# Causal attention row maxima: six reductions per group over pairs of PSUM banks in place of twelve over single banks

## The reference

```python
q = bitlinear(x, wq).reshape(B, S, N_KV, G, HEAD_DIM)
k = bitlinear(x, wk).reshape(B, S, N_KV, HEAD_DIM)
v = bitlinear(x, wv).reshape(B, S, N_KV, HEAD_DIM)
scores = jnp.einsum('bskgd,btkd->bkgst', q, k) * sm_scale
scores = jnp.where(causal, scores, -jnp.inf)
probs = jax.nn.softmax(scores, axis=-1)
out = jnp.einsum('bkgst,btkd->bskgd', probs, v)
```

## Time and profile before

| | |
|---|---|
| time, median of 3 runs | 691.62 us (690.61 to 692.38) |
| span of the profiled execution (first to last instruction) | 690.5 us |
| PE busy | 581.9 us, 84% |
| DVE busy | 451.5 us, 65% |
| ACT busy | 311.6 us, 45% |
| POOL busy | 251.7 us, 36% |
| mean granted TensorE clock | 0.938 of 2.4 GHz |

### The profile page before, as it was taken

One profiled execution on the slowest core, in us unless ns is written; L12 is line 12 of the kernel. 1 busy time (PEld: TensorE's weight loads), 2 busy tenths in 40 slices (PEclk: granted clock), 3 DMA queues, 4 the chain that ended last, 5 costly groups with the idle time before them and its releaser, 6 DMA issues.

```text
span 690.5 us, 11130 instructions
## 1 busy us (share of the span) xinstructions
PE 581.9 (84%) x3618; PEld 420.6 (61%) x3618; DVE 451.5 (65%) x881; ACT 311.6 (45%) x511; POOL 251.7 (36%) x294
## 2 busy tenths in 40 slices
PE   0358999999998897988626879998989989999994
PEld 0244544554443486766524667886768868888883
DVE  5898767877773667555888658758675464444444
ACT  1132556666676532275115563433534444444442
POOL 5821233343447314031030632443324434444440
PEclk9976599999999999999768989999999999999998
DMA  6063210111330013000020112231222222222310
GB/s 171 0 162 97 59 38 22 34 35 36 112 111 1 12 47 58 0 1 1 0 91 0 47 47 68 84 101 46 69 69 78 89 82 80 88 89 90 91 54 30
DMA packets 25627, 41.22 MB, mean 60 GB/s; under 512 B 3640, under 2 KB 17272, under 8 KB 25592
## 3 DMA queue, kind: packets, MB, share of 16 engines
q1 hardware_dynamic: 25160, 39.72, 19.5%
q0 software_dynamic: 432, 1.05, 0.9%
HBM read 37.81 MB, written 3.80 MB: 60 GB/s over the span
## 4 chain that ended last, share of the span: by engine, by line
PE 57%; DVE 25%; issue 7%; ACT 6%; POOL 3%; DMA 1%; SPq 1%; POOLq 0%; DVEq 0%; ACTq 0%
PE ps L1484 9%; PE ps L1472 7%; PE ps L1473 7%; PE ps L1474 7%; PE ps L1424 7%; PE ps L1553 6%; PE ps L1435 6%; PE ps L1427 2%; DVE st L756 2%; DVE xn L684 2%; ACT h_hi L1246 2%; DVE hf L1100 2%; DVE sg L1095 2%; PE ps L1680 1%; DVE negm L844 1%
## 5 line engine op out<-in xcount | busy, mean ns | idle before, releaser
L638 POOL TENSOR_TENSOR mslot_lo<-mraw,mslot_hi 128x768 fp32r<-128x768 f32 x60 | 112.2, 1870 | 176.7 <-ACT mslot_hi L1298 176.7
L844 DVE TENSOR_REDUCE negm<-ps 128x1 f32<-128x512 f32 (+2 forms) x192 | 107.6, 593 | 36.7 <-PE ps L1427 35.6
L1246 ACT CAST h_hi<-hf 128x512 fp32r<-128x512 f32 x76 | 47.2, 621 | 181.3 <-DVE hf L1100 144.1
L1208 ACT ACTIVATE probs<-ps 128x512 f32<-128x512 f32 x160 | 91.9, 597 | 66.7 <-PE ps L1435 66.0
L1472 PE MATMUL ps<-cols_hi,mslot_hi 128*128 128x512 f32 x240 | 96.4, 402 | 3.7 <-ACT sg L1240 2.2
L1473 PE MATMUL ps<-cols_hi,mslot_lo 128*128 128x512 f32 x240 | 94.3, 393 | 0.0
L1474 PE MATMUL ps<-cols_lo,mslot_hi 128*128 128x512 f32 x240 | 93.7, 390 | 0.0
L1095 DVE TENSOR_TENSOR sg<-sg,ps 128x512 f32<-128x512 f32 x60 | 41.0, 683 | 75.0 <-PE ps L1474 58.3
L1484 PE MATMUL ps<-mslot_hi,h_hi 128*128 128x256 f32 x240 | 78.0, 325 | 9.0 <-DVE h_lo L1104 9.0
L1424 PE MATMUL ps<-k_all,q_all 72*128 (+4 forms) x256 | 73.8, 330 | 9.2 <-DMA q_all<-q_parts_scratch 7.4
L1104 DVE TENSOR_TENSOR h_lo<-hf,h_hi 128x512 fp32r<-128x512 f32 x60 | 41.5, 692 | 41.2 <-ACT h_hi L1246 41.2
(11 more groups left out here) (221 smaller groups left out, 1176.7 us busy)
## 6 DMA issues: line engine op xcount, KB each, us to landing
mraw<-in_moe_w SPq DMA_DIRECT2D x60, 384.0 KB, 3.1
q_all<-q_parts_scratch SPq DMA_DIRECT2D x48, 96.0 KB
q_parts_scratch<-qparts SPq DMA_DIRECT2D x6, 256.0 KB, 2.5
k_parts_scratch<-kparts SPq DMA_DIRECT2D x6, 192.0 KB, 3.8
k_all<-k_parts_scratch SPq DMA_DIRECT2D x6, 192.0 KB
xa<-in_x SPq DMA_DIRECT2D x2, 512.0 KB, 4.9
w2a<-in_w SPq DMA_DIRECT2D x1, 1024.0 KB, 8.0
w1raw<-in_w SPq DMA_DIRECT2D x2, 512.0 KB, 5.4
```

Source lines behind the costliest of these rows:

```text
L638: pool.tensor_tensor(mslot_lo[:, place, :], mraw[:, place, :], mslot_hi[:, place, :].bitcast(F32), ALU.subtract)\
L844: dve.tensor_reduce(negm[:, par, qt, h0:h0 + nh], ps[:, u % 4, 0:nh * w].rearrange("p (h t) -> p h t", h=nh), AX.X, ALU.max, negate=True). ...
L1208: act.activation(probs[:, par, u, :], ps[:, 4 + u % 2, :], ACT.Exp)\
L1246: act.copy(h_hi[:, par, :], hf[:, par, :]).then_inc(h_hi_done, 1)
```

## The change

`UNITS` now has six entries, each for four heads of tiles 1 and 0 or two heads of tiles 3 and 2. PE makes them at even u only, and each fills two banks: the four banks are a ring of two pairs, and R of pair j waits until pair j-2 has been reduced. DVE makes one reduction over both banks of a pair, at even u. Everything else stands where it stood. In the loop, PE has six waits on `s1_read` fewer per slot, and DVE six waits and six reductions fewer.

```diff
-        UNITS = ([(3, h, 1) for h in range(4)] + [(2, h, 1) for h in range(4)]
-                 + [(1, 0, 2), (1, 2, 2), (0, 0, 2), (0, 2, 2)])
+        UNITS = [(3, 0, 1), (3, 2, 1), (2, 0, 1), (2, 2, 1), (1, 0, 2), (0, 0, 2)]
+        ROW_UNITS = len(UNITS)
...
-                    need(pool, s1_read, g * 12 + 12)
+                    need(pool, s1_read, (g + 1) * ROW_UNITS)
...
-                for u, (qt, h0, nh) in enumerate(UNITS):
-                    if has(n, 0):
+                for u in range(12):
+                    if has(n, 0) and u % 2 == 0:
                         g = n
+                        pair_of, (qt, h0, each) = u // 2 % 2, UNITS[u // 2]
                         if u == 0:
                             need(dve, msplit, g - 1)
-                        need(dve, s1_full, g * 12 + u + 1)
+                        need(dve, s1_full, g * ROW_UNITS + u // 2 + 1)
                         w = (qt + 1) * P
                         dve.tensor_reduce(
-                            negm[:, par, qt, h0:h0 + nh],
-                            ps[:, u % 4, 0:nh * w].rearrange("p (h t) -> p h t", h=nh),
+                            negm[:, par, qt, h0:h0 + 2 * each]
+                            .rearrange("p (k h) -> p k h", k=2),
+                            ps[:, 2 * pair_of:2 * pair_of + 2, 0:each * w]
+                            .rearrange("p k (h t) -> p k h t", h=each),
                             AX.X, ALU.max, negate=True).then_inc(s1_read, 1)
...
             def score_rows(g, u):
-                qt, h0, nh = UNITS[u]
-                need(pe, s1_read, g * 12 + u - 3)
+                qt, h0, each = UNITS[u]
+                need(pe, s1_read, g * ROW_UNITS + u - 1)
                 w = (qt + 1) * P
-                for h in range(h0, h0 + nh):
-                    c = (h - h0) * w
-                    pe.matmul(ps[:, u % 4, c:c + w],
+                for h in range(h0, h0 + 2 * each):
+                    bank, c = 2 * (u % 2) + (h - h0) // each, (h - h0) % each * w
+                    pe.matmul(ps[:, bank, c:c + w],
...
-                        score_rows(g, u)
+                        if u % 2 == 0:
+                            score_rows(g, u // 2)
```

More of the change, by code:

```diff
@@ L1418, in score_rows @@
             def score_rows(g, u):
-                qt, h0, nh = UNITS[u]
-                need(pe, s1_read, g * 12 + u - 3)
+                qt, h0, each = UNITS[u]
+                need(pe, s1_read, g * ROW_UNITS + u - 1)
                 w = (qt + 1) * P
-                for h in range(h0, h0 + nh):
-                    c = (h - h0) * w
-                    pe.matmul(ps[:, u % 4, c:c + w],
+                for h in range(h0, h0 + 2 * each):
+                    bank, c = 2 * (u % 2) + (h - h0) // each, (h - h0) % each * w
+                    pe.matmul(ps[:, bank, c:c + w],
                               q_all[0:72, bass.ds(g * (GQ * T) + (h * T + qt * P), P)],
                               k_all[0:72, bass.ds(g * T, w)], start=True, stop=False)
-                    mm = pe.matmul(ps[:, u % 4, c + w - P:c + w], identb[:, :], hide_cols[:, :],
+                    mm = pe.matmul(ps[:, bank, c + w - P:c + w], identb[:, :], hide_cols[:, :],
                                    start=False, stop=True)
@@ L1539, in slot @@
                         pe.wait_ge(att_ready, NKV)
-                        pe.wait_ge(s1_read, 12 * NG)
+                        pe.wait_ge(s1_read, ROW_UNITS * NG)
                         transposes(0, 0, att_tile(0))
```

## The result

The changed kernel takes 697.72 us (median of 4 runs, 696.05 to 698.12) beside 691.48 us of before (4 runs, 690.61 to 692.38): ratio 1.0082, 95% interval 1.0067 to 1.0098, +6.2 us. The profiled execution has a span of 696.0 us where before had 690.5, so it is 5.5 us longer.

The account below looks back on a forecast made before the run. PE was taken to bound the steady slots, DVE and PE's chain to `mrow` slots 0 and 1. Steady slots +4.0 us and the head +1.0 made +5.0 on the 691.6 median: 696.6 us, range 692.0 to 699.5.

Parts of the forecast that it names:

- What bounds the kernel: Steady slots: PE is busy 14.94 of 15 us, DVE has 3.5 us to spare; a faster DVE alone gives nothing.
- DVE's busy total: Whole kernel: a sign to look for, DVE's busy total falling by 8 to 14 us while the time does not.
- The price of a two-bank reduction: DVE: a pair of 1,024 elements costs between 1.07 and 1.20 us, taken as 1.14 start to start, 1.22 in duration.
- rival C: Pairs stop PE if a two-bank reduction lasts 1.7 us, not 1.22; at 2.4 us each, 709 us; chance 8%.
- The steady slots, +4.0 us: Slots 4 to 15 and the second cast: PE meets ACT later, 0.31 us a loop slot; bounds 1.2 and 6.5.
- R never waits for DVE from slot 2 on: PE from slot 2 on: a sign to look for, score rows never held by DVE's reductions.
- the ring's 0.4 us to spare: Tightest place, tile 3's second pair: DVE reads it until 3.4 us, R wants its banks at 3.85; cost 0.
- Slots 0 and 1, +1.0 us: Head: later Hadamard product and whole pairs delay `mrow`, so slot 2 begins at 68.5, was 67.47; bounds 0.5 and 2.2.
- less if the clock rises within it: Head: the Hadamard product takes 3.57 us at the half clock, less with a rise within it; end 58.8 to 59.3.
- 1.6 if the clock does not rise during the Hadamard product: Head: a bound on the loss in slots 0 and 1, 1.6 us where the forecast has +1.0.
- A (no change): Rival: ACT's stops do not add up, the loop keeps 9.77 us; only slots 0 and 1 cost, 692.6 us; chance 20%.
- B (PE's sequencer): Rival: PE's register work lengthens loop slots, six fewer waits per slot help; -2.8 us, 688.8 us; chance 9%.

Follow-up runs that it names:

- e2: Kernel before with only PE's order changed to two units at each even step; DVE keeps twelve single reductions: 695.76 us, ratio 1.0056.
- e1: Kernel before with only DVE's reductions made in pairs; PE keeps one unit per step: 694.90 us, ratio 1.0047.
- e3: Changed kernel with the last two heads of query tile 0 put back behind PV3: 696.67 us, ratio 1.0079.
- e7: Changed kernel with DVE's copy `v_now` moved behind the first reduction of a slot: 696.86 us, ratio 1.0077.
- e10: Kernel before with the whole change (pairs on PE and DVE) in slots 0 and 1 only: 693.24 us, ratio 1.0032.
- e4: Kernel before with the whole change from slot 2 on; slots 0 and 1 as before: 695.13 us, ratio 1.0063.
- e9: Kernel before with, up to slot 15, PV0 to PV3 at steps 5 to 8 and division, `o_cols` and `v_now` moved: 690.26 us, ratio 0.9988.
- e5: Changed kernel with the Hadamard product of slot 0 one step earlier, ahead of the fourth pair: 697.82 us, ratio 1.0087.
- e6: Kernel before with DVE's reductions in pairs, PE's old order, and `v_now` moved behind a slot's first reduction: 694.41 us, ratio 1.0042.
- e8: Kernel before with PV0 to PV3 at steps 5 to 8 and the division behind the third reduction: 702.72 us, ratio 1.0132.

## Why the prediction was right, step by step

**The time and the sign** were right: 696.6 us forecast, 697.72 measured, in the range of 692.0 to 699.5. In the traces the steady slots cost 0.4 us less than forecast and the head 1.5 more; that the two errors have opposite signs is luck.

**What bounds the kernel** was right. PE is as full as before in the loop (40.00 of 40.18 us in four slots, 38.91 of 39.17 before) while DVE gave back 2.0 us in them; a faster DVE bought nothing. DVE's busy total was to fall by 8 to 14 us and fell by 5.8: too much was forecast. The prediction's own 0.4 us a slot makes only 6.4 in 16 slots; the 8 to 14 fits single durations, but back-to-back reductions overlap by 0.1 us each and the page counts overlapped time once. Also, the sixteen `v_now` copies took 1.2 us more than before.

**The price of a two-bank reduction**, "no cheaper than its elements, no dearer than two instructions", held: 1.22, 0.94 and 0.69 us. With it rival C, pairs that stop PE at 1.7 us a reduction, fell.

**The steady slots, +4.0 us.** Measured 3.6. The mechanism is shown by e2, where PE's order alone gives 10.04 us slots, and e1, where its absence gives 9.78. That these meeting points are with ACT is read from the traces (the waits, the place of C4 behind C2's exponent) and from e3, which takes one of them away; no run made ACT itself faster. The places, forecast and measured: OT 0.96 and 0.88; C3 3.26 and 3.23; C4 3.60 and 3.59 (its weights); R behind C4 at 3.85 and 4.01; PV0 5.25 and 5.22. A loop slot costs 0.25 to 0.27 instead of 0.31. OT started 0.06 us behind the end of `o_cols` and not the 0.14 that was read behind the exponent, but those 0.08 are nearly gone at C3; the difference is 0.03 us at PV0 and 0.01 behind it. The written-out slots cost 0.37 instead of 0.31, the slots of the long casts 0.46 and 0.24 where 0.4 and 0.2 were forecast.

**"R never waits for DVE from slot 2 on"** was wrong in a detail: two waits, 1.7 us together from 102 to 200 us, fewer than the ten (5.4 us) that the same view gives for before. Both, and the two more that follow by 240 us, are in written-out slots behind the loop, and two short ones (0.4 us together) come before it, in slots 2 and 3; in the loop the ring's 0.4 us to spare held.

**Slots 0 and 1, +1.0 us.** This term was mis-sized: slot 2 began 2.46 us later, beyond even the 2.2 of its bounds. Of these, 0.15 us had come before slot 0 (the first R starts at 51.30, before at 51.15). Three more kernels, e3, e7 and e10, have the same instructions of PE and DVE in slots 0 and 1 as after, and the clock did not rise at the same time in their traces:

| kernel | clock rises at | falls again at | `mrow` starts | slot 2 begins | later than before |
|---|---|---|---|---|---|
| e3 | 58.4 | 65.3 | 65.25 | 68.91 | 1.45 |
| e10 | 59.3 | 66.2 | 65.56 | 69.21 | 1.75 |
| after | 60.2 | 63.6 | 66.27 | 69.92 | 2.46 |
| e7 | 60.1 | 63.5 | 66.33 | 69.99 | 2.53 |

e3 is the case that the prediction reckoned with, a rise within the product at 58.4 (58.3 before). It has +1.45, so 0.45 us of the miss are the walk's own: DVE could read the pair of tile 1 at 59.93 and not at 59.6, and `mrow` starts at 65.25 where the walk had 64.83. The other 1.0 us came with the clock, in two ways. First, "less if the clock rises within it": in after it stayed at 0.50 until 60.2. So the product ended at 59.34, the rows of tile 1 behind it were made at the half clock too, and DVE had their pair at 60.64. The prediction had named this case, "1.6 if the clock does not rise during the Hadamard product", and kept it as a bound; e10, where the clock rose just behind the product, has 1.75. Second, the clock fell again at 63.6, so MT at 63.80 and the third pair behind it were slow, and DVE waited 0.28 us more. The head of before moves with the clock as well: in e4 and e9, which have that head, the clock rose at 56.1 and 56.2, and slot 2 began at 66.59 and 66.61 and not at 67.46. How far after's trace had a late rise by chance is not shown; e10, 2.2 us in the median of twelve runs, is the better measure of this term.

The cause is also only in part where the prediction had it, in the product's later place. e1 and e2 have the product at nearly the same place, 55.30 and 55.15, and the rise of the clock at 58.4 and 58.7; e2, with single reductions, lost 0.17 us to slot 2 and e1, with pair reductions, 1.56. In e1 R of tile 2 waits for DVE's first pairs, which has the product end 0.63 us later than before, and from its end to `mrow` it takes 6.69 us where before has 5.75. A reduction that starts when its second bank is full, and frees the first with it, is what the head pays for. Where the reductions are pairs the product's place counts too: in e5 it starts 1.36 us earlier than in after and slot 2 begins 1.86 earlier, the earlier rise of the clock included.

**The rivals.** A (no change) fell because ACT's stops did add up, in every slot. B (PE's sequencer) fell too: R's "issue" waits went from 15.6 to 12.1 us, but C's from 2.4 to 9.1, and e2, with all twelve waits on `s1_read`, has the same 10.04 us slots as after.

Against the rule of the Trainium skill, Perfetto Trace Analysis, "Optimizing Scalar/DVE Operations", that the prediction cited: grouping can help where the engine is saturated. Slots 0 and 1 have such a stretch, ten reductions without a stop, and e10 lost 2.2 us with pairs on PE and DVE there alone; in e1, with DVE's grouping alone, slot 2 began 1.56 us later. What was grouped was also the hand-over, and DVE's saved 0.4 us a slot was less than the wait for whole pairs. The measurement decides against the rule here.

**What the forecast lacked** is the port that DVE and POOL share. It cost e1 1.1 us and e2 0.7 us in each of two slots, e3 0.9 in the first of them, and was hidden in after.

**Left open:** why the clock's steps in slots 0 to 3 lie some 4 us apart from kernel to kernel (the last rise at 86.9 in e4, 91.1 in e5), why the rise in slot 0 moves even where slots 0 and 1 are the same (58.4 in e3, 60.2 in after), and what a given head would cost at a fixed clock. No run here holds the clock still.

## What to carry to other kernels

When a change groups work on an engine with slack, look past that engine: it also sets the order of its producer and the size of what is handed over at once, and here PE, whose own work stayed the same, paid 0.25 us a slot at its meeting points with a third engine. Walk one period of the bottleneck engine by starts, not by durations, and price every place where it answers another engine. A two-bank reduction is cheap; waiting for its second bank is not, least of all at the head of a pipeline where the producer is slow.

## What the runs showed of the hardware

- A DVE copy of 128x128 fp32 from SBUF to SBUF lasts 0.21 to 0.29 us in most slots (0.61 at most, in e6, beside a shorter instruction of POOL), and 1.06 us (after, at 227.44) to 2.26 us (e8, at 183.65) when it begins while POOL's 128x1024 `tensor_tensor` runs; it ends when POOL does. Before has one such copy too, 1.07 us at 222.91, beside `w3lo`. When the copy begins first, neither is longer (0.28 and 2.35).
- A reduction over two PSUM banks lasts 1,224 ns for 1,024 elements, the same within 2 ns for two rows as for four.
- PE followed ACT's `o_cols` by 0.06 us in the loop of after, and an exponent by 0.14 in that of before.
- Behind slot 4 the clock still falls to 0.50 for some microseconds, in most traces and at different places (188.1 in e3, 215.3 in before, 227.5 in after). It costs the slot that it falls in some 1.6 us: between PV0 of slots 16 and 17 before has 12.41, after 12.32, e1 and e5 12.36 and 12.42, and e2, e3, e4, e6 and e7 10.82 to 10.85. Single slots of two traces are compared only where both had the full clock.
